# A fused layer (projections, attention, expert layer) on one core: the first attention group's operands loaded during the projections, and most of the expert choice made there too

## The chip, the cores and the metric

One Trainium2 chip, one core of it. The metric is the device time of one execution in microseconds (us). It is given as the median over runs of the same kernel; one further execution was recorded by the hardware profiler, and all rows of the trace come from that one.

## What is computed

```python
xn = _layernorm(x, axis=-1)                     # x: 16 x 1024 x 256
s = _L0_attn_ref(xn, W_q, W_k, W_v, W_o)        # 16 heads of 16, rope on q and k, causal softmax
g = _silu(_L0_ffn_ref(xn, w_router, w_fc, w_proj))
x = x + s * g
# in _L0_ffn_ref:
logits = jnp.einsum('bsd,ed->bse', x, w_router)       # 8 experts
indices = jnp.argmax(softmax(logits), axis=-1)        # the first of the largest
onehot = jax.nn.one_hot(indices, NUM_EXPERTS)
```

Every token goes to one expert out of eight, the first that has its largest logit.

## The kernel before

The program has three stages, each in a block of its own; at the end of a block all engines wait for each other.

**Projections** (`project_phase`). The 16384 tokens are 32 tiles (t) of 512 tokens, and each tile is 4 subtiles of 128 tokens, 128 subtiles (n) in all. For each tile: ScalarE (ACT) applies the layer norm (`apply`, L278), TensorE (PE) transposes, ACT and VectorE (DVE) cut the result in two parts (`xT_hi` L286, `xT_lo` L354). For each subtile PE makes v, the eight logits (ps_vr) and q, k (ps_qk) in three passes each; DVE does the rope products (L385 to L387), GpSimd (POOL) adds them (L263), PE transposes the sum, and ACT, DVE and POOL cut it in three bf16 parts (`part1` L300, `take_rest` L395, `part2` L306, `part3` L252). q and k leave for DRAM as `parts_dram`, v as `v_dram`, the normed tokens as `xn_dram`, and zeros go to `xs_dram`.

The order on each engine is written out by hand. All these transfers are issued by SyncE (SP), in one loop over tiles: store xn of t+1, load x of t+4, one or two stores of zeros, wait for v of t, store it (L203, 4 transfers), wait for `part3` of t, store the parts (L206, 4 transfers). Most buffers are double: ACT's v copy for tile t waits for the v store of tile t-2 (`v_stored`), and `part1` for tile t waits for the parts store of tile t-2 (`parts_stored`). DVE's loop does, for subtile n: `xT_lo` of the next tile when n is a tile's last subtile, `rope_parts(n)`, `ln_stats`, `take_rest(n-2)`, and at a tile's last subtile the layer norm's means and variances, from which POOL makes the factors that `apply` waits for.

After the loop DVE chooses the experts of all 16384 tokens in one go (L415 to L426: largest logit, which experts equal it, their numbers, the lowest, a 0/1 table `onehot`). PE counts from `onehot`, and DVE works out each token's place in the sorted order (L432 to L467, to `slot` and `block_expert`). With that the block ends.

**Attention** (`attention_phase`). 64 groups (16 batches by 4 groups of 4 heads), with operand buffers q_st, k_st, v_st in a ring of four. `load(b, r)` brings one group's operands with 13 transfers: 6 for q and 6 for k, each of 16 partitions and 128 KB, and one of 512 KB over 128 partitions for v. At the block's start SP issues the loads of groups 0, 1 and 2, and then `load_max(0, 0, 0)`, which waits for the first maxima. PE waits for POOL's constants (`a_consts`) and for group 0's 13 transfers, and then forms the 32 row blocks of group 0 (L947), whose maxima DVE takes (L855); the steady loop over groups begins after them. POOL's setting of ones in k_st is waited for only after those 32.

**Experts and output** (`expert_output_phase`) is untouched.

## Time and profile before

| | us |
|---|---|
| median of 3 runs (lowest, highest) | 2686.38 (2682.7, 2691.24) |
| the profiled execution: its time | 2684.91 |
| the profiled execution: span of the trace | 2683.2 |
| projections: last PE matmul of the loop ends at about | 408.2 |
| DVE chooses experts, then places | 409.44 to 430.46 |
| attention's block: SP's first load is issued at | 430.75 |
| PE's first matmul of attention | 446.19 |
| steady loop over the 64 groups begins | 473.91 |
| last exponential of attention begins | 2290.6 |
| PE busy, DVE busy over the span | 94%, 80% |

How to read it: times within the trace count from the span's start. The profiled execution's time is 1.7 us more than its span (work around it that no row shows). The page's second part gives, for 40 equal slices of the span, each engine's busy share and TensorE's granted clock; the seventh slice (402 to 470) holds the passage from the projections to attention: PE falls to 3 tenths there, ACT to 0 and the granted clock to 5 tenths. A row with L and a number names the line of the kernel; PEld is PE's weight load, SPq the issuing of a transfer by SP.

### The profile page before, as it was taken

To read this page: it belongs to the slowest core of one execution; us is meant where nothing else is said; L and a number is where in the kernel's file an instruction comes from. 1 tells how busy PE (TensorE), PEld (TensorE's weight loads), DVE (VectorE), ACT (ScalarE), POOL (GpSimd) and SP (SyncE) were. 2 spreads that over 40 slices of the span, in tenths; PEclk is the share of its full clock that TensorE was granted. 3 is DMA by queue.
4 is the path that set the end of the run, shared out by engine and by line. 5 is a ranking of instruction groups with operands and counts; after the bars stand their busy time and mean duration, and the time that the engine had idled before them with its cause. 6 is when DMAs were issued, how large, how long until landed. Compare 5 with 4: busy or idle time off the path is not lost. (4 is left out here: it accounts for less than half of the span.)

```text
span 2683.2 us, 53569 instructions
## 1 busy us (share of the span) xinstructions
PE 2528.3 (94%) x16877; PEld 1271.1 (47%) x16877; DVE 2135.9 (80%) x6183; ACT 1781.9 (66%) x4187; POOL 990.7 (37%) x1189
## 2 busy tenths in 40 slices
PE   7999993999999999999999999999999999799587
PEld 6888781333333333333333333333333333588476
DVE  7888886888888888888888888888888887354244
ACT  5777770677777777777777777777777777455111
POOL 6888883222222222222222222222222222222664
PEclk9999995999999999999999999999999999899798
DMA  6999998456465465454554554654655640697797
GB/s 235 351 350 354 347 336 184 98 103 121 88 111 105 91 111 110 95 115 94 101 122 88 106 110 88 111 112 94 112 98 99 116 96 24 214 307 260 234 339 253
DMA packets 305865, 435.04 MB, mean 162 GB/s; under 512 B 101808, under 2 KB 204464, under 8 KB 305584
## 3 DMA queue, kind: packets, MB, share of 16 engines
q1 hardware_dynamic: 293296, 398.05, 57.6%
q0 software_dynamic: 12288, 33.57, 5.4%
q8 instruction: 136, 2.23, 0.4%
q14 instruction: 145, 1.19, 0.2%
HBM read 241.18 MB, written 188.74 MB: 160 GB/s over the span
## 5 line engine op out<-in xcount | busy, mean ns | idle before, releaser
L855 DVE CUSTOM_DVE_ANT_0 dump<-ps_rows,mask 128x512 bf16<-128x512 f32 (+7 forms) x2048 | 1481.0, 754 | 223.8 <-issue 184.3
L834 ACT ACTIVATE probs<-ps_cols 128x512 f32<-128x512 f32 (+3 forms) x3072 | 1315.7, 495 | 514.2 <-PE ps_cols L1003 504.0
L1003 PE MATMUL ps_cols<-q_st,k_st 99*128 99x512 bf16 (+3 forms) x3072 | 863.0, 329 | 5.5 <-DMA q_st<-max_T 3.3
L813 POOL TENSOR_SCALAR_AFFINE_SELECT probs<-probs 128x512 f32<-128x512 f32 x512 | 325.9, 636 | 1363.1 <-ACT probs L834 1363.1
L947 PE MATMUL ps_rows<-k_st,q_st 96*128 96x512 bf16 (+3 forms) x3072 | 781.5, 330 | 29.8 <-DMA v_st<-v_dram 22.1
L979 PE MATMUL ps_ctx<-probs,v_st 128*32 128x512 f32 (+3 forms) x6144 | 654.5, 498 | 1.5 <-POOL probs L813 1.2
L1003 PEld LDWEIGHTS ps_cols<-q_st,k_st 99*128 99x128 bf16 x3072 | 279.7, 97 | 590.4 <-ACT probs L834 380.3
L947 PEld LDWEIGHTS ps_rows<-k_st,q_st 96*128 96x128 bf16 x3072 | 265.3, 98 | 326.8 <-DVE row_max L855 128.0
L979 PEld LDWEIGHTS ps_ctx<-probs,v_st 128*32 128x32 f32 x6144 | 120.8, 108 | 206.2 <-issue 103.0
L263 POOL TENSOR_TENSOR roped<-rope_c,rope_s 128x512 f32<-128x512 f32 x128 | 164.9, 1288 | 41.8 <-DVE rope_s L387 41.8
L855 DVE DVE_READ_ACCUMULATOR2_ANT row_max<- 128x1 f32 x2048 | 168.2, 82 | 0.2
L1295 PE MATMUL ps_t<-w_o_sb,cT 128*128 128x256 f32 x512 | 130.8, 408 | 38.4 <-issue 22.3
L1165 POOL DMA_INDIRECT gate<-g_dram,slot x128 | 127.8, 998 | 74.5 <-issue 36.3
L252 POOL TENSOR_TENSOR parts<-rest,parts 128x512 bf16<-128x512 f32 x128 | 149.4, 1168 | 1.2 <-ACT parts L306 1.2
L1236 DVE TENSOR_TENSOR prod<-ps_t,gate 128x512 f32<-128x512 f32 x64 | 43.0, 688 | 133.8 <-remote 74.8
L1206 ACT ACTIVATE cT<-ps_t 128x512 f32<-128x512 f32 x64 | 34.9, 598 | 168.4 <-remote 86.5
L800 POOL DMA_INDIRECT xs_dram<-xn_sb,slot x128 | 124.5, 973 | 31.3 <-issue 31.3
L1295 PEld LDWEIGHTS ps_t<-w_o_sb,cT 128*128 128x128 f32 x512 | 102.6, 205 | 57.2 <-issue 27.9
L395 DVE TENSOR_TENSOR rest<-ps_m,parts 128x512 f32<-128x512 f32 x128 | 87.3, 682 | 47.5 <-ACT parts L300 46.4
L485 PE MATMUL ps_qk<-w_all_hi,xT_hi 128*128 128x512 f32 x256 | 101.9, 398 | 0.0
L485 PE MATMUL ps_vr<-w_all_hi,xT_hi 128*128 128x264 f32 x256 | 84.7, 331 | 18.0 <-DVE xT_lo L354 17.9
L485 PE MATMUL ps_qk<-w_all_lo,xT_hi 128*128 128x512 f32 x256 | 101.6, 397 | 0.0
(115 smaller groups left out, 2639.5 us busy)
## 6 DMA issues: line engine op xcount, KB each, us to landing
parts_dram<-parts SPq DMA_DIRECT2D x128, 384.0 KB, 3.9
q_st<-parts_dram SPq DMA_DIRECT2D x384, 128.0 KB
k_st<-parts_dram SPq DMA_DIRECT2D x384, 128.0 KB
v_dram<-v_sb SPq DMA_DIRECT2D x128, 256.0 KB, 5.4
v_st<-v_dram SPq DMA_DIRECT2D x64, 512.0 KB
xs_dram<-zeros SPq DMA_DIRECT2D x36, 512.0 KB, 7.0
xs_sb<-xs_dram SPq DMA_DIRECT2D x72, 256.0 KB, 4.5
g_dram<-g_sb SPq DMA_DIRECT2D x72, 256.0 KB, 3.4
```

The costliest lines, as they stand in the source:

```text
L252: nc.gpsimd.tensor_tensor(parts[:, t % 2, :, 2, s * P:(s + 1) * P], rest[:, n % RR].rearrange("p (b t) -> p b t", b=4), parts[:, t % 2, :, ...
L263: nc.gpsimd.tensor_tensor(roped[:, n % RR, :], rope_c[:, n % 2, :], rope_s[:, n % 2, :], ALU.add).then_inc(roped_ready, 1)
L485: mm = nc.tensor.matmul(out, lhs(i, c), rhs(j, c), start=((c, i, j) == PASSES[0]), stop=((c, i, j) == PASSES[-1]))
L800: pool.indirect_dma_start(out=xs_dram[:, :], out_offset=bass.IndirectOffsetOnAxis(ap=token_row[:, s:s + 1], axis=0), in_=xn_sb[:, u, s % S ...
L813: nc.gpsimd.affine_select(out=tri, in_=tri, compare_op=ALU.is_ge, fill=0.0, base=0, pattern=[[0, GH], [1, P]], channel_multiplier=-1).then ...
L834: nc.scalar.activation(probs[:, k % PB, h, 0:w], ps_cols[(GH * k + h) % CB][:, 0:w], ACT.Exp).then_inc(exp_done, 1)
L855: nc.vector.tensor_tensor_reduce(out=dump[:, even, 0:n], in0=ps_rows[:, 512 * bank:512 * bank + n], in1=mask[:, S - n:S], scale=1.0, scala ...
L947: mm = nc.tensor.matmul(ps_rows[:, 512 * (bank + c):512 * (bank + c) + w], q, k_st[r][0:KS, c, h * 512:h * 512 + w], start=True, stop=True)
L979: mm = nc.tensor.matmul(ps_ctx[VW * h:VW * (h + 1), o:o + w], v_st[r][:, j, VW * h:VW * (h + 1)], probs[:, k % PB, h, 0:w], start=(j == 0) ...
L1003: nc.tensor.matmul(ps_cols[(GH * k + h) % CB][:, 0:w], k_st[r][:, j // IB, h * 512 + (j % IB) * P:h * 512 + (j % IB + 1) * P], q_st[r][:, ...
L1165: pool.indirect_dma_start(out=gate[:, r, s, :], out_offset=None, in_=g_dram[:, :], in_offset=bass.IndirectOffsetOnAxis(ap=token_row[:, t * ...
L1295: mm = nc.tensor.matmul(ps_y[u][i][:, (s % 2) * D:(s % 2 + 1) * D], cT[:, u, c, s * P:(s + 1) * P], w_o_sb[:, c, :], start=(c == 0), stop= ...
```

## The change

Two things are moved, both out of the passage between the two blocks.

1. Group 0's operand buffers (`q_st0`, `k_st0`, `v_st0`) and their semaphore live for the whole program. SP issues group 0's 13 loads in the projections' loop, in the pass for tile 8, between that tile's v stores and its parts stores; it first waits until the stores of tiles 0 and 1 are done. At the start of attention's block SP issues only the loads of groups 1 and 2. Before the first block ends SP waits for group 0's loads.
2. The expert choice is a helper `choose(i, lo, hi, done)` of five steps. The steps for subtiles 0 to 111 (the first 28 tiles) are put into DVE's loop, one after each `take_rest` of subtiles 112 to 116; the steps for the last 16 subtiles come after the loop. `onehot` is now written expert by expert, so that its innermost run is contiguous.

```diff
+def load_operands(sp, parts_dram, v_dram, b, r, q, k, v, loaded):
+
+    for a, (dst, slots) in enumerate(((q, SLOT_Q), (k, SLOT_K))):
+        for slot, part in enumerate(slots):
+            src = parts_dram[:, 2 * a + r // 2, part, (r % 2) * GW:(r % 2 + 1) * GW, :].rearrange(
+                "(b c) (d h) t -> b d c (h t)", c=TPB, h=GH)[b]
+            sp.dma_start(dst[slot * HD:(slot + 1) * HD], src).then_inc(loaded, 16)
+    src = v_dram[:, r].rearrange("(b c) p n -> b p c n", c=TPB)[b]
+    sp.dma_start(v[:].rearrange("p (c s) n -> p c (s n)", c=TPB), src).then_inc(loaded, 16)
...
+    FIRST_GROUP_AT = 8
+    EARLY = (NT - 4) * SUB
+    CHOICE = 5
+    ROUTED = 1 + 2 * CHOICE
...
+            if t == FIRST_GROUP_AT:
+                for j in range(TPB):
+                    sp.wait_ge(v_stored[j % 2], 16 * NG * (j // 2 + 1))
+                    sp.wait_ge(parts_stored[j % 2], 64 * (j // 2 + 1))
+                load_operands(sp, parts_dram, v_dram, 0, 0, *first_in)
             sp.wait_ge(part3_done, SUB * (t + 1))
...
+        sp.wait_ge(first_in[3], LOAD)
         sp.wait_ge(xs_cleared, 16 * CLEARS)
...
+        nc.vector.tensor_scalar_add(ids_low[:], ids_sb[:], -float(E)).then_inc(route, 1)
+
+        def choose(i, lo, hi, done):
+
+            w = hi - lo
+            ids = ids_low[:].unsqueeze(1).broadcast_to((P, w, E))
+            dve.wait_ge(route, done)
+            if i == 0:
+                dve.wait_ge(logits_ready, hi)
+                nc.vector.tensor_reduce(best[:, lo:hi], logits[:, lo:hi], axis=mybir.AxisListType.X,
+                                        op=ALU.max).then_inc(route, 1)
+            elif i == 1:
+                nc.vector.tensor_tensor(is_best[:, lo:hi], logits[:, lo:hi],
+                                        best[:, lo:hi].unsqueeze(2).broadcast_to((P, w, E)),
+                                        ALU.is_equal).then_inc(route, 1)
+            elif i == 2:
+                nc.vector.tensor_tensor(is_best[:, lo:hi], is_best[:, lo:hi], ids, ALU.mult).then_inc(route, 1)
+            elif i == 3:
+                nc.vector.tensor_reduce(first_best[:, lo:hi], is_best[:, lo:hi], axis=mybir.AxisListType.X,
+                                        op=ALU.min).then_inc(route, 1)
+            else:
+                nc.vector.tensor_tensor(onehot[:, :, lo:hi], first_best[:, lo:hi].unsqueeze(1).broadcast_to((P, E, w)),
+                                        ids_low[:].unsqueeze(2).broadcast_to((P, E, w)),
+                                        ALU.is_equal).then_inc(route, 1)
...
             if n >= LAG:
                 take_rest(n - LAG)
+            if EARLY <= n - 2 < EARLY + CHOICE:
+                choose(n - 2 - EARLY, 0, EARLY, 1 + n - 2 - EARLY)
...
+        for i in range(CHOICE):
+            choose(i, EARLY, NS, 1 + CHOICE + i)
...
-        for r in range(RING - 1):
+        for r in range(1, RING - 1):
             load(0, r)
```

The removed lines of the choice are in the kernel above (L414 to L428). Nothing else is changed but numbers of semaphore waits.

How the order moves, at the three places that the prediction speaks of. The line numbers after the change are higher by the lines added above.

**SP in the projections, the pass for tile 8.** Before, from that tile's v stores (L203) to the next tile's:

```order
L203 DMA v_dram<-v_sb 128x512 x4
L206 DMA parts_dram<-parts 128x3x512 x4
L175 DMA xn_dram<-xn 128x1024
L172 DMA x_sb<-in_x_dram 128x4x256
L178 DMA xs_dram<-zeros 128x1024
L203 DMA v_dram<-v_sb 128x512 x4
```

Now:

```order
L231 DMA v_dram<-v_sb 128x512 x4
L79 DMA q_st<-parts_dram 16x2x2048 x6
L79 DMA k_st<-parts_dram 16x2x2048 x6
L81 DMA v_st<-v_dram 128x2x512
L239 DMA parts_dram<-parts 128x3x512 x4
L203 DMA xn_dram<-xn 128x1024
L200 DMA x_sb<-in_x_dram 128x4x256
L206 DMA xs_dram<-zeros 128x1024
L231 DMA v_dram<-v_sb 128x512 x4
```

Thirteen transfers stand ahead of tile 8's parts stores, in the same queue.

**DVE in the projections, end of tile 28 and tile 29** (xT_lo is what PE waits for at a tile's start). Now, from the first choice step on:

```order
L442 TENSOR_REDUCE best<-logits 128x112
L388 TENSOR_TENSOR xT_lo<-ps_f,xT_hi 128x512 x2
...
L429 TENSOR_TENSOR rest<-ps_m,parts 128x512
L445 TENSOR_TENSOR is_best<-logits,best 128x896
L377 BN_AGGR mv<-stats 128x2 x4
...
L429 TENSOR_TENSOR rest<-ps_m,parts 128x512
L449 TENSOR_TENSOR is_best<-is_best,ids_low 128x896
...
L429 TENSOR_TENSOR rest<-ps_m,parts 128x512
L451 TENSOR_REDUCE first_best<-is_best 128x112
...
L429 TENSOR_TENSOR rest<-ps_m,parts 128x512
L454 TENSOR_TENSOR onehot<-first_best,ids_low 128x8x112
L388 TENSOR_TENSOR xT_lo<-ps_f,xT_hi 128x512 x2
```

Five instructions are new there: one ahead of xT_lo of tile 29, one ahead of the means (BN_AGGR) of tile 30, and three more ahead of xT_lo of tile 30. Before, none of them stood there.

**DVE after the projections' loop.** Before:

```order
L395 TENSOR_TENSOR rest<-ps_m,parts 128x512 x3
L415 TENSOR_REDUCE best<-logits 128x128
L416 TENSOR_SCALAR ids_low<-ids_sb 128x8
L418 TENSOR_TENSOR is_best<-logits,best 128x1024
L421 TENSOR_TENSOR is_best<-is_best,ids_low 128x1024
L424 TENSOR_REDUCE first_best<-is_best 128x128
L426 TENSOR_TENSOR onehot<-first_best,ids_low 128x128x8
L432 CAST sub_total<-ps_f 128x8
```

Now:

```order
L429 TENSOR_TENSOR rest<-ps_m,parts 128x512 x3
L442 TENSOR_REDUCE best<-logits 128x16
L445 TENSOR_TENSOR is_best<-logits,best 128x128
L449 TENSOR_TENSOR is_best<-is_best,ids_low 128x128
L451 TENSOR_REDUCE first_best<-is_best 128x16
L454 TENSOR_TENSOR onehot<-first_best,ids_low 128x8x16
L479 CAST sub_total<-ps_f 128x8
```

The same five steps remain, over an eighth of the elements; ids_low has left.

## Rows read from the trace of the kernel before

**Rows 1.** The page, busy time of each engine over the span

```profile
PE 2528.3 (94%) x16877; PEld 1271.1 (47%) x16877; DVE 2135.9 (80%) x6183; ACT 1781.9 (66%) x4187; POOL 990.7 (37%) x1189
```

**Rows 2.** Windows: from:to, length, busy PE PEld DVE ACT POOL, PEclk, DMA share, GB/s

```profile
137.93:150.10 12.17, 11.65 (x73) 9.86 (x73) 10.67 (x29) 8.88 (x23) 10.81 (x11) 1.00 1.03 367
```

**Rows 3.** Timeline after the projections: start, duration, engine, line, operation [idle before]

```profile
407.43 4.49 POOL L252 TENSOR_TENSOR parts<-rest,parts 128x512 bf16<-128x512 f32 x4
...
409.44 1.21 DVE L415 TENSOR_REDUCE best<-logits 128x128 f32<-128x1024 f32 x1
...
410.87 2.13 DVE L418 TENSOR_TENSOR is_best<-logits,best 128x1024 f32<-128x1024 f32 x1
413.03 1.22 DVE L421 TENSOR_TENSOR is_best<-is_best,ids_low 128x1024 f32<-128x1024 f32 x1
...
415.54 4.70 DVE L426 TENSOR_TENSOR onehot<-first_best,ids_low 128x1024 bf16<-128x1024 f32 x1
...
430.23 0.23 DVE L467 CAST slot<-best 128x128 uint32<-128x128 f32 x1
```

**Rows 4.** Timeline, the last stores and the start of attention's block

```profile
413.97 3.25 SPq L206 DMA_DIRECT2D parts_dram<-parts  x4
...
430.75 2.67 SPq L727 DMA_DIRECT2D q_st<-parts_dram  x6
...
432.64 0.29 POOL L789 TENSOR_SCALAR_AFFINE_SELECT ident_b<-ident_b 128x128 bf16<-128x128 bf16 x1
...
446.19 6.89 PE L947 MATMUL ps_rows<-k_st,q_st 96*128 96x512 bf16 x16 [22.11 <-DMA v_st<-v_dram]
...
471.37 0.95 SPq L739 DMA_DIRECT2D q_st<-max_T  x1
```

**Rows 5.** Windows: group 0's q and k loads, then its v load

```profile
431.60:443.90 12.30, 0.00 (x0) 0.00 (x0) 0.00 (x0) 0.00 (x0) 12.09 (x10) 0.50 1.04 141
443.90:445.50 1.60, 0.00 (x0) 0.00 (x0) 0.00 (x0) 0.00 (x0) 1.60 (x1) 0.50 1.23 355
```

**Rows 6.** Timeline of SP's queue, the pass for tile 8

```profile
132.01 3.96 SPq L203 DMA_DIRECT2D v_dram<-v_sb  x4
138.34 2.34 SPq L206 DMA_DIRECT2D parts_dram<-parts  x4
```

**Rows 7.** Timeline of ACT in tile 10: v copy, part1 of its first subtile

```profile
141.04 0.39 ACT L319 ACTIVATE v_sb<-ps_vr 128x256 f32<-128x256 f32 x1 [1.90 <-DMA v_dram<-v_sb]
...
147.09 0.60 ACT L300 ACTIVATE parts<-ps_m 128x512 bf16<-128x512 f32 x1 [0.30 <-PE ps_m L494]
```

**Rows 8.** Timeline of tile 25, from its first PE matmul to that of tile 26

```profile
320.35 0.39 PE L485 MATMUL ps_vr<-w_all_hi,xT_hi 128*128 128x264 f32 x1 [0.46 <-DVE xT_lo L354]
...
325.55 0.38 ACT L319 ACTIVATE v_sb<-ps_vr 128x256 f32<-128x256 f32 x1 [3.99 <-DMA v_dram<-v_sb]
...
333.88 0.39 PE L485 MATMUL ps_vr<-w_all_hi,xT_hi 128*128 128x264 f32 x1 [0.48 <-DVE xT_lo L354]
```

**Rows 9.** Windows: the granted clock (PEclk) after the projections

```profile
411.00:413.00 2.00, 0.00 (x0) 0.00 (x0) 2.00 (x1) 0.00 (x0) 0.92 (x1) 0.50 1.06 429
446.00:454.00 8.00, 6.99 (x18) 1.92 (x19) 6.77 (x32) 0.00 (x0) 0.86 (x1) 0.50 1.06 136
474.00:475.00 1.00, 1.00 (x3) 0.34 (x4) 0.00 (x0) 0.44 (x1) 0.00 (x0) 0.50 0.88 352
478.00:479.00 1.00, 1.00 (x8) 0.35 (x6) 1.00 (x6) 0.73 (x2) 0.49 (x1) 0.73 0.00 0
```

**Rows 10.** Timeline of DVE, small and contiguous operations of the placing

```profile
420.91 1.23 DVE L435 TENSOR_TENSOR before_sub<-earlier,sub_total 128x1024 bf16<-128x1024 bf16 x1
...
423.49 0.22 DVE L444 TENSOR_TENSOR lower_n<-lower_e,n_blocks 128x64 f32<-128x64 f32 x1
423.75 0.22 DVE L447 TENSOR_REDUCE first_block<-lower_n 128x8 f32<-128x64 f32 x1
```

**Rows 11.** Timeline, start of tile 29: DVE's xT_lo and PE's first matmul

```profile
369.01 1.28 DVE L354 TENSOR_TENSOR xT_lo<-ps_f,xT_hi 128x512 fp32r<-128x512 f32 x2
...
370.34 0.39 PE L485 MATMUL ps_vr<-w_all_hi,xT_hi 128*128 128x264 f32 x1 [0.47 <-DVE xT_lo L354]
```

More of the change, by code:

```diff
@@ L412, in _ @@
                 ln_variance(t + 2)
-        dve.wait_ge(logits_ready, NS)
-        nc.vector.tensor_reduce(best[:], logits[:], axis=mybir.AxisListType.X, op=ALU.max).then_inc(route, 1)
-        nc.vector.tensor_scalar_add(ids_low[:], ids_sb[:], -float(E)).then_inc(route, 1)
-        dve.wait_ge(route, 2)
-        nc.vector.tensor_tensor(is_best[:], logits[:], best[:].unsqueeze(2).broadcast_to((P, NS, E)),
-                                ALU.is_equal).then_inc(route, 1)
-        dve.wait_ge(route, 3)
-        nc.vector.tensor_tensor(is_best[:], is_best[:], ids_low[:].unsqueeze(1).broadcast_to((P, NS, E)),
-                                ALU.mult).then_inc(route, 1)
-        dve.wait_ge(route, 4)
-        nc.vector.tensor_reduce(first_best[:], is_best[:], axis=mybir.AxisListType.X, op=ALU.min).then_inc(route, 1)
-        dve.wait_ge(route, 5)
-        nc.vector.tensor_tensor(onehot[:].rearrange("p e s -> p s e"),
-                                first_best[:].unsqueeze(2).broadcast_to((P, NS, E)),
-                                ids_low[:].unsqueeze(1).broadcast_to((P, NS, E)), ALU.is_equal).then_inc(route, 1)
-        ROUTED = 6
+        for i in range(CHOICE):
+            choose(i, EARLY, NS, 1 + CHOICE + i)
         dve.wait_ge(totals_ready, 1)
@@ L519, in _ @@
                 transpose_qk(n - LAG)
-        pe.wait_ge(route, 6)
+        pe.wait_ge(route, ROUTED)
         pe.wait_ge(consts_ready, CONSTS)
@@ L534, in _, with attention_phase @@
                              start=False, stop=True).then_inc(ranks_ready, 1)
-def attention_phase(nc, ctx, parts_dram, v_dram, ctx_dram, xn_dram, xs_dram, token_row):
+def attention_phase(nc, ctx, parts_dram, v_dram, ctx_dram, xn_dram, xs_dram, token_row, first_in):
     def sb(name, shape, dt=F32):
@@ L556, in attention_phase @@
     RING = NG
-    KM = KS + PARTS
     HALVES = S // 512
     IB = 512 // P
-    q_st = [sb(f"q_st{r}", [KM, HALVES, GH * 512], BF16) for r in range(RING)]
-    k_st = [sb(f"k_st{r}", [KM, HALVES, GH * 512], BF16) for r in range(RING)]
-    v_st = [sb(f"v_st{r}", [P, NB, GH * VW]) for r in range(RING)]
+    q_st = [first_in[0]] + [sb(f"q_st{r}", [KM, HALVES, GH * 512], BF16) for r in range(1, RING)]
+    k_st = [first_in[1]] + [sb(f"k_st{r}", [KM, HALVES, GH * 512], BF16) for r in range(1, RING)]
+    v_st = [first_in[2]] + [sb(f"v_st{r}", [P, NB, GH * VW]) for r in range(1, RING)]
     mask = sb("mask", [P, S])
@@ L586, in attention_phase @@
     ones_set = sem("ones_set")
-    operands_loaded = [sem(f"operands_loaded{r}") for r in range(RING)]
+    operands_loaded = [first_in[3]] + [sem(f"operands_loaded{r}") for r in range(1, RING)]
     slot_ready = sem("slot_ready")
@@ L713, in attention_phase @@
     block = ctx.enter_context(nc.Block())
-    LOAD = 16 * (2 * len(SLOT_Q) + 1)
     SUBS_SCATTERED = NT * SUB // N
@@ L720, in load @@
         def load(b, r):
-            done = operands_loaded[r]
-            for a, (dst, slots) in enumerate(((q_st[r], SLOT_Q), (k_st[r], SLOT_K))):
-                for slot, part in enumerate(slots):
-                    src = parts_dram[:, 2 * a + r // 2, part, (r % 2) * GW:(r % 2 + 1) * GW, :].rearrange(
-                        "(b c) (d h) t -> b d c (h t)", c=TPB, h=GH)[b]
-                    sp.dma_start(dst[slot * HD:(slot + 1) * HD], src).then_inc(done, 16)
-            src = v_dram[:, r].rearrange("(b c) p n -> b p c n", c=TPB)[b]
-            sp.dma_start(v_st[r][:].rearrange("p (c s) n -> p c (s n)", c=TPB), src).then_inc(done, 16)
+            load_operands(sp, parts_dram, v_dram, b, r, q_st[r], k_st[r], v_st[r], operands_loaded[r])
         def load_max(n, r, c):
@@ L1332, in gated_attention @@
         token_row, block_expert = routing_tables(nc, whole)
+        first_in = first_operands(nc, whole)
         with ExitStack() as ctx:
             project_phase(nc, ctx, x_t, w_all, rope, expert_ids, parts_dram, v_dram, xn_dram, xs_dram,
-                          (token_row, block_expert))
+                          (token_row, block_expert), first_in)
         with ExitStack() as ctx:
-            attention_phase(nc, ctx, parts_dram, v_dram, ctx_dram, xn_dram, xs_dram, token_row)
+            attention_phase(nc, ctx, parts_dram, v_dram, ctx_dram, xn_dram, xs_dram, token_row, first_in)
         with ExitStack() as ctx:
```

14 lines of the change are left out of this document (11 added, 3 removed).

## The prediction

> **What bounds the kernel now.** I read the page first: PE is busy 94% of the span [rows 1], so a gain has to come from a stretch where PE stands idle, and anything that delays PE inside a dense stretch is paid in full. Then the windows: in tile 10 of the projections PE is busy 11.65 of 12.17 us, DVE 10.67, POOL 10.81, and the DMA share is 1.03 at 367 GB/s [rows 2]. So PE sets the pace there and everything else, the DMA engines too, has little to spare. Then the timeline of the passage: DVE begins the choice at 409.44, and its last operation ends at 430.46 (430.23 + 0.23) [rows 3]; SP's first load goes out at 430.75, and PE's first matmul of attention starts at 446.19 with "DMA v_st<-v_dram" as the releaser of its wait [rows 4]. These are two serial pieces of 21 and 15.4 us with PE nearly idle, and the change takes something from both. What it takes it puts into the dense stretch, so the question is what it costs there.
>
> **The load, where it leaves.** Without group 0's load PE starts when POOL's constants are ready, 432.64 + 0.29 = 432.93, which is 2.2 us after the block's start instead of 15.4. **Saved: 446.19 - 432.93 = 13.2 us.** What comes next is not late: the 32 row blocks and the copy of the maxima take 471.37 - 446.19 = 25.2 us whatever starts them [rows 4], so SP would issue the first maxima at 2.2 + 25.2 = 27.4 us after the block's start, and the loads of groups 1 and 2, 13.9 us each (below), would end at 0.85 + 27.8 = 28.6. That bounds a new wait by 1.2 us; I take 0, since the maxima's transfer itself is small.
>
> **The load, where it arrives.** Its price on the DMA engines: q and k pass from 431.60 to 443.90 at 141 GB/s with the share at 1.04, v from 443.90 to 445.50 at 355 GB/s [rows 5]. So the load fills all engines for 12.3 + 1.6 = 13.9 us, though it is only 2.1 MB; at the 367 GB/s of tile 10 it would be 5.7 us. The twelve q and k transfers, of 16 partitions each, are the slow ones. One page explains it: the Trainium skill, "SBUF — State Buffer", section "Door 1: The DMA port swizzle", says that a transfer reaches only the ports that its partitions belong to, that 16 partitions reach 4 of 16 ports, about 109 GB/s. The trace agrees in kind, with 141 where the page has 109 (successive transfers go to other partitions). By the page's figure alone the load would hold the engines 16.0 us and my sum would come out 2.1 us later.
>
> In the changed kernel these 13 transfers are issued behind tile 8's v stores, which end at 132.01 + 3.96 = 135.97 [rows 6], in the one queue that SP has. Those v stores have landed at 141.04, when ACT's wait for them ends [rows 7], so the engines are at the new load between 136 and 140; I take 138.5 and get 152.4 for its end. Tile 8's parts stores (issued at 138.34 before [rows 6]; 1.6 MB, 4 us at 367 to 400 GB/s) come next and land, with 1 us that I allow for the end of a store, at 157.4. `part1` of tile 10 waits for them, and it started at 147.09 [rows 7]. **ACT is held for 10.3 us.** Nothing on ACT can pass it: behind it stand xT_hi of tile 11 and the v copies, and PE waits for xT at every tile's start even now (0.47 us [rows 11]), so PE loses 10.3 too. Such lateness is handed on: in tile 25 the v store came late, ACT waited 3.99 us [rows 8] instead of 1.90 [rows 7], and the tile took 333.88 - 320.35 = 13.5 us [rows 8] instead of 12.2. Bounds: 7.5 us if the load starts at 136 and shares a little with the stores, 13 us if it starts at 140 and later v stores are late too. SP's own issuing, 6 us for 13 transfers at 2.67 us for six [rows 4], lies beneath this.
>
> The clock adds to it. PE's last matmul of the projections ended at about 408.2 and from 411 on the granted clock is 0.50, 1.2 GHz [rows 9]. After PE starts in earnest at 473.9 it stays at 0.50 and is back at 2.4 GHz within the window 478 to 479 (0.73) [rows 9]: 4.4 us at half speed, 2.2 us of work lost. A stall of 10 us will do the same to a stage that PE bounds: **2.2 us**, between 0 (the stall falls in pieces) and 11.7 (a whole tile at half speed, below).
>
> Load in all: -13.2 + 10.3 + 2.2 = **-0.7 us**.
>
> **The choice, where it leaves.** It took 420.24 - 409.44 = 10.8 us. Five steps over 16 subtiles (128 elements a partition) remain. Neighbouring steps over 64 elements start 0.26 us apart (423.49, 423.75 [rows 10]); a further 64 elements add 0.07 by the 1.22 us of 1024 [rows 3], so five steps are 1.7 us. The 4.70 us of `onehot` [rows 3] belonged to its scattered bf16 writing; contiguous, the like operation took 1.23 us [rows 10], and I count `onehot` as an ordinary step. But POOL is in its last four L252 until 411.92, and the same rows show what that does [rows 3]: is_best, with two inputs in SBUF, was on the engine from 410.87 for 2.13 us and ended at 413.00, which is 1.08 after POOL's end; the mult of the same size after it took 1.22. The reduce before it (one input) ran its usual 1.21 beside POOL. In the new order two such steps meet POOL, so I take 2.8 us instead of 1.7 (ends: 1.7, and 3.8 if DVE waits for all four). **Saved: 10.8 - 2.8 = 8.0 us** (7.0 to 9.1). The 10.2 us of placing are unchanged, so the block ends near 422.8 on the old clock; SP's last stores, issued by 417.22 [rows 4], are done a few us later and stay just ahead.
>
> **The choice, where it arrives.** Five steps over 896 elements, 7/8 of 1.22 less the overlap of neighbours, 1.0 us each: 5.0 us of DVE work in tiles 28 and 29. At 369.01 DVE begins xT_lo of tile 29 directly after a `rest`, and PE, at 370.34, had waited 0.47 us for it [rows 11]. The first step stands exactly before it, the second before the means that POOL and ACT wait for before PE's next transposes, the other three before xT_lo of tile 30, in a stretch where DVE has no gap. So I count them as paid in full, 5.0 us. Three have two SBUF inputs and meet POOL, which is busy 10.81 of 12.17 us [rows 2]: from 0 to 1.2 us for each (the 1.05 that is_best lost beside POOL [rows 3] is one such), I take 0.5: 1.5 us. The same page, section "Who interferes with whom", has it that the pair of ports is held for a whole instruction and that POOL is stopped by DVE as well; no row here shows that side. **Paid: 6.5 us** (5.0 to 8.6). ids_low at the start (0.3 us) lies under PE's first matmuls: 0.
>
> Choice in all: -8.0 + 6.5 = **-1.5 us**.
>
> **Sum:** -0.7 - 1.5 = -2.2 us on the profiled execution's 2684.9, 2682.7. The median of the runs lies 1.5 above that execution, so I forecast **2684.2 us**. With all ends together: -13.2 + 7.5 + 5.0 - 9.1 = -9.8, and -13.2 + 13 + 2.2 + 8.6 - 7.0 = +3.6, so 2676.6 to 2690.0. A measurement of this kernel tells about 0.3% (8.1 us) from no change.
>
> **Rivals.**
> - *The load hides.* If the engines are not as full as a share of 1.03 says (ACT waits 1.90 us for a v store without harm [rows 7], and tile 10's 367 GB/s is below the 429 of 411 to 413 [rows 9]), or if stores pass while q and k wait on the receiving side, PE loses some 2 us and the clock stays up: -13.2 + 2 - 1.5 = -12.7, **2673.7**. Such a reading has a page behind it: the Trainium skill, "DMA: Bandwidth & Descriptors", section "Anatomy of one DMA — SWDGE (gpsimd) path", fits 436 GB/s plus about 2 us for a transfer (on POOL's path), which would make the load 4.8 us of engine time, hence nearly free. Against it stands 141 GB/s at a full share with nothing else running [rows 5]. Chance 0.22.
> - *The early steps of the choice hide, the rest as forecast.* If DVE's lateness falls into gaps behind tile 30, where the statistics end, only 1 of 6.5 us is paid: 2684.2 - 5.5 = **2678.7**. Against: PE does not get lost time back, having no gaps. Chance 0.10.
> - *The clock stays down* (slower). In the row blocks PE ran at 0.50 for 28 us though busy 6.99 of 8 us [rows 9]. If the stall in tile 11 leaves PE at 1.2 GHz and waits for late v stores keep it there, each tile costs 11.7 us more [rows 2]. With one and a half tiles: -13.2 + 10.3 + 17.5 - 1.5 = +13.1, **2699.5**. It decides against the change by more than 8.1 us from about one tile on. Against: at half speed PE is busy without a break, as at 474, where the clock came back in 4.4 us. Chance 0.10.
> - *Forecast:* chance 0.58.
>
> **Numbers.** Faster by over 0.3%: the load hiding (0.22), part of the second rival (0.04), and the low tail of the forecast (0.05), 0.31. Slower: the clock (0.10) and a tail of 0.01, 0.11. The same: 0.58. The range reaches down to 2672 to take in most of the first rival, and up to 2692; outside are the clock's case and the deeper part of the hiding, some 2 in 10.
>
> **What would show it.** In the changed kernel's trace: the first L947 matmul 2.2 us after SP's first load of the block (else step one is wrong); ACT's L300 of tile 10 idle some 10 us for "DMA parts_dram" and a tile of over 20 us there, with a granted clock of 0.50 after it (if the tile is under 15 us, the load hides); tiles 28 and 29 together 5 to 8.6 us longer; from the first late choice step to PE's count 1.7 to 3.8 us. The forecast is wrong if the sum of the projections' lengthening is under 10 or over 25 us.

## The result, and the profile after

The changed kernel takes 2681.88 us (median of 20 runs, 2678.71 to 2687.96) against 2686.81 (20 runs, 2680.96 to 2691.24) for the kernel before in the same comparison: a ratio of 0.9984 with a 95% interval from 0.9977 to 0.9992, 0.16% or some 4 us less. The interval leaves out 1, so the gain is there, but it is small: it lies within the 0.3% that the prediction calls "the same", and 2.3 us below the forecast of 2684.2. Its profiled execution has a span of 2678.4 us, 4.8 less than before.

The page, busy time of each engine over the span, reads as before [rows 1]; no engine's work has grown by more than 2.2 us:

```profile
PE 2527.3 (94%) x16876; PEld 1272.4 (48%) x16877; DVE 2136.9 (80%) x6188; ACT 1782.4 (67%) x4187; POOL 992.9 (37%) x1189
```

**Where the load arrives.** The timeline of SP's queue, the pass for tile 8 (against [rows 6]):

```profile
130.52 3.75 SPq L231 DMA_DIRECT2D v_dram<-v_sb  x4
134.45 3.83 SPq L79 DMA_DIRECT2D q_st<-parts_dram  x6
138.33 2.76 SPq L79 DMA_DIRECT2D k_st<-parts_dram  x6
141.13 0.43 SPq L81 DMA_DIRECT2D v_st<-v_dram  x1
141.60 2.66 SPq L239 DMA_DIRECT2D parts_dram<-parts  x4
```

ACT in tile 10 (against [rows 7]):

```profile
139.51 0.39 ACT L353 ACTIVATE v_sb<-ps_vr 128x256 f32<-128x256 f32 x1 [1.85 <-DMA v_dram<-v_sb]
...
152.19 0.60 ACT L334 ACTIVATE parts<-ps_m 128x512 bf16<-128x512 f32 x1 [6.88 <-DMA parts_dram<-parts]
```

Windows (the columns of [rows 2]): first over the times of [rows 2], then while q and k pass, then after them:

```profile
137.93:150.10 12.17, 10.16 (x64) 8.40 (x63) 7.34 (x22) 5.14 (x13) 9.48 (x9) 1.00 1.06 279
...
138.30:146.30 8.00, 7.95 (x54) 6.84 (x53) 6.50 (x20) 5.14 (x13) 7.55 (x8) 1.00 1.04 227
146.30:152.20 5.90, 1.84 (x11) 1.28 (x9) 0.47 (x2) 0.01 (x1) 1.55 (x2) 0.92 1.08 391
```

PE's first matmul of tile 11, and the granted clock during its wait:

```profile
155.17 0.59 PE L532 MATMUL ps_vr<-w_all_hi,xT_hi 128*128 128x264 f32 x1 [7.03 <-DVE xT_lo L388]
```

```profile
151.00:152.00 1.00, 0.00 (x0) 0.00 (x0) 0.00 (x0) 0.00 (x0) 0.00 (x0) 0.63 1.03 402
152.00:153.00 1.00, 0.00 (x0) 0.00 (x0) 0.18 (x1) 0.81 (x2) 0.00 (x0) 0.50 1.07 390
```

What to see: 13 issues stand before the parts stores, and these go out at 141.60. Counted from PE's first matmul of tile 10 (137.93 before, 136.46 now) that is 5.1 us, where it was 0.4: 4.7 us late. (The traces are 1.5 us apart: tile 0 took 12.0 us instead of 13.3, and the loop began 0.2 us earlier. Tile 0 takes 12.0 to 13.4 in executions of kernels that don't differ there.) Then their landing takes a median of 7.7 us from the issue instead of 4.2. ACT was ready at 145.3 and waits 6.88 us, and PE, which needs the next tile's xT, waits 7.03. The DMA share stays over 1 in these windows, but with q and k in the queue only 227 GB/s pass; from 146.3 on it is 391 again. From first matmul to first matmul tile 10 takes 18.71 us and tile 11 13.17, where all their neighbours take 12.15: 6.56 + 1.02 = 7.6 us.

**Where the choice arrives.** Timeline, DVE in tiles 28 and 29:

```profile
374.24 1.07 DVE L442 TENSOR_REDUCE best<-logits 128x112 f32<-128x896 f32 x1
...
378.61 1.47 DVE L445 TENSOR_TENSOR is_best<-logits,best 128x896 f32<-128x896 f32 x1
...
384.27 1.08 DVE L449 TENSOR_TENSOR is_best<-is_best,ids_low 128x896 f32<-128x896 f32 x1
...
387.46 1.07 DVE L451 TENSOR_REDUCE first_best<-is_best 128x112 f32<-128x896 f32 x1
...
390.63 1.46 DVE L454 TENSOR_TENSOR onehot<-first_best,ids_low 128x896 bf16<-128x896 f32 x1
392.01 1.28 DVE L388 TENSOR_TENSOR xT_lo<-ps_f,xT_hi 128x512 fp32r<-128x512 f32 x2
```

POOL beside them, two rows of part3 (the second is of the usual length):

```profile
384.32 2.07 POOL L286 TENSOR_TENSOR parts<-rest,parts 128x512 bf16<-128x512 f32 x1
...
387.95 1.17 POOL L286 TENSOR_TENSOR parts<-rest,parts 128x512 bf16<-128x512 f32 x1
```

PE's three waits that follow, then windows of the clock around the last:

```profile
376.56 0.39 PE L532 MATMUL ps_vr<-w_all_hi,xT_hi 128*128 128x264 f32 x1 [1.46 <-DVE xT_lo L388]
...
382.71 0.93 PE L524 MATMUL ps_f<-ident,xn 128*128 128x128 f32 x4 [1.19 <-ACT xn L312]
...
393.34 0.39 PE L532 MATMUL ps_vr<-w_all_hi,xT_hi 128*128 128x264 f32 x1 [3.70 <-DVE xT_lo L388]
```

```profile
390.00:392.00 2.00, 0.00 (x0) 0.00 (x0) 2.00 (x3) 0.91 (x2) 2.00 (x2) 1.00 0.00 0
392.00:394.00 2.00, 0.66 (x4) 0.66 (x5) 2.00 (x5) 0.00 (x0) 1.11 (x1) 0.90 0.00 0
394.00:396.00 2.00, 2.00 (x8) 1.71 (x8) 1.97 (x10) 0.45 (x2) 1.28 (x1) 0.50 1.05 368
396.00:398.00 2.00, 2.00 (x12) 1.68 (x11) 0.71 (x3) 0.55 (x2) 1.81 (x3) 0.74 1.09 385
```

The five steps take 6.15 us on DVE. The three steps with two SBUF inputs meet POOL: is_best and onehot are stretched to 1.47 and 1.46, and beside mult and onehot POOL's addition needs 2.07 and 2.01 us instead of 1.17. PE, for want of xT_lo, waits 1.46 instead of 0.47, then 1.19 for the normed tokens, then 3.70; after that its granted clock is 0.50 (1.2 GHz) for some 3 us. Tiles 28, 29 and 30 take 13.14, 16.78 and 13.40 us: 6.9 us more.

**Where both leave.** Timeline of DVE after the loop (against [rows 3]), and of POOL's last part3:

```profile
421.57 0.28 DVE L442 TENSOR_REDUCE best<-logits 128x16 f32<-128x128 f32 x1
421.89 1.19 DVE L445 TENSOR_TENSOR is_best<-logits,best 128x128 f32<-128x128 f32 x1
423.11 1.12 DVE L449 TENSOR_TENSOR is_best<-is_best,ids_low 128x128 f32<-128x128 f32 x1
...
424.59 0.29 DVE L454 TENSOR_TENSOR onehot<-first_best,ids_low 128x128 bf16<-128x128 f32 x1
```

```profile
419.55 4.54 POOL L286 TENSOR_TENSOR parts<-rest,parts 128x512 bf16<-128x512 f32 x4
```

The start of attention's block, and its first stretch (against [rows 4]):

```profile
435.40 2.66 SPq L79 DMA_DIRECT2D q_st<-parts_dram  x6
...
437.64 6.91 PE L977 MATMUL ps_rows<-k_st,q_st 96*128 96x512 bf16 x16 [8.92 <-POOL ident_b L819]
437.65 13.89 POOL L824 MEMSET k_st<- 3x4096 bf16 x4
...
447.06 1.03 DVE L898 TENSOR_SCALAR max_parts<-row_max 128x16 bf16<-128x16 f32 x1
448.28 0.17 DVE L901 SCALAR_TENSOR_TENSOR max_rest<-row_max,max_parts 128x16 f32<-128x16 f32 x1
449.52 2.05 DVE L905 TENSOR_SCALAR max_parts<-max_rest 128x16 bf16<-128x16 f32 x1
...
466.23 0.59 PE L1033 MATMUL ps_cols<-q_st,k_st 99*128 99x512 bf16 x1 [3.29 <-DMA q_st<-max_T]
```

The late choice takes 3.31 us instead of 10.8: two of its five steps take four times as long as the others; the second ends at 424.23, just after POOL's four end at 424.09. PE's first matmul comes 2.24 us after SP's first load, instead of 15.4. From it to the steady loop it is 28.59 us, where before it was 27.75; that 0.84 us is new and has a cause of its own (e10).

The balance at the start of the steady loop, 473.94 before and 466.23 now: tile 0 -1.3 (it varies, see above), tiles 10 and 11 +7.6, tile 25 -0.9 (unexplained: 13.5 us before, 12.6 here, 13.4 in e1, 12.15 in e3), tiles 28 to 30 +6.9, choice -7.5, PE's start in the block -13.2, first stretch +0.8, the start of the program -0.2; together -7.8, and 7.7 is what the rows give. Of these 7.7 us the span keeps 4.8. Attention takes 1819.1 us instead of 1818.3, and from its last copy to the end 393.1 instead of 391.0, in code that was not touched. Over nine profiled executions (before, the change, e1 to e3, e6, e10 to e12) attention takes 1817.8 to 1819.2 and the rest 388.9 to 394.5. So a trace shows the passage term by term, and the whole to no better than some 5 us.

### The profile page after: what moved, and what is told of

Read it like the earlier page. It is cut to its first block and busy times, and to the rows that moved or that the text cites. A ratio compares the mean times of both kernels' runs of the same rounds, so it can differ in the third digit from the quotient of the medians.

```text
span 2678.4 us, 53577 instructions
## 1 busy us (share of the span) xinstructions
PE 2527.3 (94%) x16876; PEld 1272.4 (48%) x16877; DVE 2136.9 (80%) x6188; ACT 1782.4 (67%) x4187; POOL 992.9 (37%) x1189
## 3 DMA queue, kind: packets, MB, share of 16 engines
q14 instruction: 146, 1.19, 0.2%
## 5 line engine op out<-in xcount | busy, mean ns | idle before, releaser
L312 ACT ACTIVATE xn<-x_sb,shift,rstd 128x256 f32<-128x256 f32 x128 | 69.8, 597 | 49.9 <-POOL shift L257 49.9
```

## The experiments

My theories after the result: (a) the load's stall is smaller than forecast because narrow transfers pass faster among the stores than at the block's start, and it grows with them; its rival, that bytes or issuing set it; (b) the choice's steps cost their own time plus POOL's; (c) both costs are ones of place, and go if the same work is put elsewhere.

All these kernels but e2, e5 and e12 make the whole choice after the loop, with the new layout of `onehot` ("choice late" below):

```diff
-            if EARLY <= n - 2 < EARLY + CHOICE:
-                choose(n - 2 - EARLY, 0, EARLY, 1 + n - 2 - EARLY)
...
-            choose(i, EARLY, NS, 1 + CHOICE + i)
+            choose(i, 0, NS, 1 + i)
```

**e1_load_only**: the load as in the change, choice late.

> Part 1 of the change alone: group 0's load in the pass for tile 8; all five steps of the choice stay behind the loop, over all 128 subtiles, in the changed form (ids_low early, onehot written in contiguous runs). My theory: tiles 10 and 11 are longer by 7.6 us together as in the changed kernel, PE starts attention 2.2 us after the block's start (13.2 us saved), and the choice takes about 7.0 us instead of 10.8, since the 4.70 us of onehot came from its scattered writing. Sum -13.2 + 7.6 + 0.9 - 3.8 = -8.5 us against before, about 2678. Rival: the moving of the choice is what brings the gain and the load nets nothing beyond its stall, onehot stays at 4 us: then 10 us of choice and about -5 us.

Measured: 2677.90 us (8 runs), ratio 0.9972 [0.996, 0.9984]. Tiles 10 and 11 take 19.55 and 14.34, 9.6 us more; ACT waits 7.71. The late choice takes 7.07 us, and `onehot` in it 1.22. The steady loop begins at 465.73, level with the change. So the load is the half that gains, and without any early step the choice is already 3.7 of 10.8 us shorter: 3.5 by `onehot` (4.70 to 1.22) and the rest by the early ids_low. The stall is 2 us longer than in the change, though the code at tile 8 is the same: one trace of a stall tells its length to no better than that.

**e2_choice_only**: the choice as in the change; all three loads at attention's start.

```diff
-            if t == FIRST_GROUP_AT:
...
-                load_operands(sp, parts_dram, v_dram, 0, 0, *first_in)
...
-        for r in range(1, RING - 1):
+        for r in range(RING - 1):
```

> Part 2 alone: the choice for 28 tiles inside the loop, group 0's load at the start of attention as before. My theory: tiles 28 to 30 are longer by about 6.9 us together and the choice behind the loop is shorter by 7.5, -0.6 us, no change that can be told. The wait for xT_lo at tile 30 is about 3.7 us and the granted clock falls to 0.50 after it. Rival: the lengthening of tiles 28 to 30 in the changed kernel came from the transfers moved, not from DVE: then those tiles stay at 12.2 us and the kernel gains 7.5.

Measured: 2686.19 us (11 runs), ratio 0.9997 [0.9988, 1.0007]. Tiles 28 to 30 take 13.14, 16.77 and 13.27, 6.7 us more, and the late choice takes 3.3: part 2 earns nothing that the times can tell. Its first stretch of attention is 27.75 us.

**e3_load_spread**: one of the 13 transfers in each pass for tiles 8 to 20, choice late.

```diff
-            if t == FIRST_GROUP_AT:
+            if FIRST_GROUP_AT <= t < FIRST_GROUP_AT + LOAD // 16:
...
-                load_operands(sp, parts_dram, v_dram, 0, 0, *first_in)
+                load_operands(sp, parts_dram, v_dram, 0, 0, *first_in, only=t - FIRST_GROUP_AT)
```

> As e1, but the 13 transfers are issued one per tile, in the passes for tiles 8 to 20. My theory: the engines have about 1.4 us to spare in each tile, a transfer of 128 KB over 16 partitions takes about 1 us of them, so ACT never waits for a parts store and all tiles from 8 on stay at 12.2 us: -13.2 + 0.9 - 3.8 = -16 us against before, about 2670. Rival: the engines have nothing to spare (their share is 1.0), the 13.9 us are paid in small pieces, 13 tiles are longer by 0.5 to 1 us each, and the time is that of e1 or worse.

Measured: 2667.34 us (5 runs), ratio 0.9935 [0.9922, 0.9948]; a second set of the same kernel (e11, below) gave 0.9935 again. The window of tile 10, in e3:

```profile
137.93:150.10 12.17, 11.65 (x73) 9.81 (x73) 10.67 (x29) 8.88 (x23) 10.79 (x10) 1.00 1.02 368
```

It is that of before [rows 2]. The same 2.1 MB, in thirteen pieces, cost nothing that the rows of e3 show: every tile after the first takes 12.15 us (in e11 and e10, with the same spread load, a tile or two among the thirteen takes 12.3 to 12.4), and the steady loop begins at 455.69, 18.3 us earlier than before.

**e6_wide**: in the pass for tile 8, twelve transfers of 128 KB and one of 512 KB over 128 partitions into spare buffers; the real load stays at attention's start, choice late. It loads 2.1 MB more than needed.

```diff
-                load_operands(sp, parts_dram, v_dram, 0, 0, *first_in)
+                for i in range(12):
+                    sp.dma_start(spare[:, i], v_dram[i // 8, i // 2 % 4, :, i % 2 * 256:i % 2 * 256 + 256])...
+                sp.dma_start(spare_v[:]..., src)...
```

> In the pass for tile 8, 12 transfers of 128 KB over 128 partitions (rows of v) and one of 512 KB, into spare buffers, stand where the changed kernel has group 0's 13; the real load is at the start of attention as before, the choice as in e1. Bytes and number of transfers are those of the load, only the partitions differ. My theory (the narrow transfers hold the engines): the load passes at 350 to 400 GB/s in about 5.7 us, and tiles 10 and 11 are longer by at most 2.5 us. Rival (what counts is SP's issuing of 13 transfers, which sends tile 8's parts store off 4.7 us later, or the bytes alone): tiles 10 and 11 are longer by 6 to 7.6 us as in the changed kernel.

Measured: one execution, 2691.21 us. Tiles 10 and 11 take 18.66 and 13.28, 7.6 us more: a stall as long as that of the change, with transfers that reach all partitions. My theory (a) fell for the size. ACT, SP's queue and windows, in e6:

```profile
152.42 0.60 ACT L339 ACTIVATE parts<-ps_m 128x512 bf16<-128x512 f32 x1 [6.83 <-DMA parts_dram<-parts]
```

```profile
135.29 5.66 SPq L239 DMA_DIRECT2D spare<-v_dram  x12
...
141.47 3.58 SPq L244 DMA_DIRECT2D parts_dram<-parts  x4
```

```profile
138.00:142.00 4.00, 3.95 (x24) 3.02 (x22) 2.98 (x12) 1.54 (x4) 3.71 (x5) 1.00 1.02 344
142.00:146.00 4.00, 4.00 (x29) 3.69 (x30) 3.52 (x8) 3.59 (x10) 3.81 (x4) 1.00 0.94 261
```

The share falls below 1 here, and 128 KB every 0.47 us is 278 GB/s: SP's issuing may let the engines run dry. That is argued, not shown, for such dips come without the load too (222 GB/s at a share of 0.84 in the window 145 to 146 before). Nor does e6 test the partitions alone: its pieces are rows of 1 KB, where q's and k's are of 4 KB, and it passes at 261 to 344 GB/s and not at the 367 of the stage. What it shows is that transfers over all partitions do not make the stall go away.

**e13_four**: the same bytes as four transfers of 512 KB, to tell issuing from bytes (the diff is against e6).

```diff
-                for i in range(12):
...
+                for i in range(4):
+                    src = v_dram[:, i].rearrange("(b c) p n -> b p c n", c=TPB)[0]
+                    sp.dma_start(spare[:, i], src).then_inc(spare_loaded, 16)
```

> As e6 (the real load stays at attention's start), but the 2.1 MB behind tile 8's v stores are four transfers of 512 KB over 128 partitions instead of thirteen, so SP needs about 0.45 us each, 1.8 us, where e6 needed 6.1 us and the change 7.1 us. If SP's issuing sets the stall, tile 8's parts stores go out only 1.8 us later than without a load; what is left is the 2.1 MB at the 367 GB/s of the stage, 5.7 us less about 1.4 us that part1 had to spare: ACT waits 4 to 4.5 us for them in tile 10, and tile 10 takes 16 to 16.5 us. The rival is that the bytes ahead of the parts stores cost the same however they are issued (the landing of the stores sets it, 6.8 us of wait in e6 and 6.9 in the change): then tile 10 takes 18.5 us again.

Measured: one execution, 2690.11 us. SP and ACT, in e13:

```profile
135.12 2.88 SPq L239 DMA_DIRECT2D spare<-v_dram  x4
138.03 4.06 SPq L242 DMA_DIRECT2D parts_dram<-parts  x4
...
149.26 0.60 ACT L337 ACTIVATE parts<-ps_m 128x512 bf16<-128x512 f32 x1 [3.18 <-DMA parts_dram<-parts]
```

Tile 10 starts at 137.22 here, so the parts stores go out 0.8 us after it, only 0.4 later than before and not 1.8: SP had stood idle from 135.97 to 138.34 before [rows 6], and four issues fit into that. They land after a median of 8.4 us, with 2.1 MB ahead of them in the queue. ACT waits 3.18 us, below the 4 to 4.5 expected, and tiles 10 and 11 take 15.02 and 13.40, 4.1 us more. In rough terms the waits add up: by the lateness of the first issue, the median landing and some 1.4 us that part1 has to spare (an estimate), 0.4 + 4.2 - 1.4 = 3.2 here, and 4.7 + 3.5 - 1.4 = 6.8 in the change. For e6 the same sum gives 4.3 + 2.3 - 1.4 = 5.2, where 6.83 was measured, so it is no law. Of the 7.6 us for thirteen transfers 3.5 are gone when the same bytes are issued in four; the other 4.1 are the bytes and the slower clock after the stall. The 3.5 us are more than the 2 us by which e1 and the change differ, but they rest on one trace each, and e13's rows are of 2 KB and not 1 or 4: how much is issuing and how much the form of the transfers is not separated.

**e7_double**: e1 with twelve more narrow transfers behind the load, into spare buffers (1.6 MB more than needed).

```diff
+                for a in range(2):
+                    for slot, part in enumerate((SLOT_Q, SLOT_K)[a]):
...
+                        sp.dma_start(spare[slot * HD:(slot + 1) * HD, a], src).then_inc(spare_loaded, 16)
```

> As e1, with twelve more transfers of 16 partitions and 128 KB behind the thirteen in the pass for tile 8, the same q and k parts again into a spare buffer. What the second dozen adds is its price without any slack. If narrow transfers hold the engines as long as at attention's start (12.3 us for twelve), tiles 10 and 11 get longer by another 12 us, 21 in all. If they pass faster in the projections (e1's trace has about 215 GB/s while they pass), another 7 to 8 us, 17 in all. If, as in e6, only bytes count (1.57 MB at 385 GB/s), another 4 us.

Measured: one execution, 2651.39 us, with the kernel before at 2648.28 in that comparison. (The chip of that comparison ran the kernel before 1.4% faster: granted clock 0.981, not 0.972. e5, e8 and e9 are from it too. Their times are compared by ratio only; the undisturbed tiles take 12.15 us there as well.) Tile 10 takes 27.13 and tile 11 13.23: 16.1 us more than undisturbed, 6.5 more than e1 and 8.5 more than the change, nearest to the 17 of the second case. ACT and a window, in e7:

```profile
161.93 0.60 ACT L341 ACTIVATE parts<-ps_m 128x512 bf16<-128x512 f32 x1 [15.29 <-DMA parts_dram<-parts]
```

```profile
139.50:155.50 16.00, 9.92 (x63) 8.24 (x62) 7.10 (x21) 5.13 (x13) 9.21 (x9) 0.96 1.05 204
```

Here the 24 narrow transfers, with v's 512 KB among them, fill the queue for 16 us: 204 GB/s at a full share, against 141 of [rows 5]. At 204 GB/s twelve would take 7.7 us. Twelve more cost 6.5 to 8.5 us, where SP needs 5.8 us to issue them, so for the narrow ones passing is probably the limit once enough are queued; the difference is within the 2 us of e1 and the change.

**e9_half**: q's six transfers in the pass for tile 8, the other seven one each in tiles 20 to 26, choice late.

> Only the six q transfers in the pass for tile 8, the other seven one per tile in the passes for tiles 20 to 26. With a fixed slack of some 3.5 us between the parts store's landing and part1, and 8.7 us for thirteen transfers, six take 3.7 us and the stall nearly vanishes: tiles 10 and 11 longer by 0 to 1.5 us. If instead a stall is in proportion to the transfers, 3.5 us.

Measured: one execution, 2634.74 us. ACT waits 3.06 us for the v store (1.90 in [rows 7]) and 1.14 for the parts; tiles 10 and 11 take 13.42 and 12.48, 1.6 us more, at the slack's 0 to 1.5 and not at the 3.5 of mere proportion. Six cost 1.6, thirteen 7.6 to 9.6, 25 16.1: a slack, then 0.9 to 1.1 us for each, and further on 0.5 to 0.7.

**e8_tail**: the 13 transfers are issued behind tile 31's parts stores and the block's end does not wait for them, choice late.

```diff
+        load_operands(sp, parts_dram, v_dram, 0, 0, *first_in)
...
-        sp.wait_ge(first_in[3], LOAD)
```

> The load goes behind tile 31's parts stores, at the end of the projections' block, which does not wait for it; the choice as in e1. My theory: the engines are free from about 420 on, while DVE chooses and places, so no tile gets longer; at 141 GB/s the load ends about 14 us later, at 434, and PE starts attention there instead of at 446.2: with the choice shorter by 3.8 us the block starts at 427 and PE waits another 7 us for the load. -12 us against before. If the load is as quick as in e1 (about 9 us), -16 us. Rival: it holds up something of the block's end, or the loads of groups 1 and 2 behind it delay the maxima: -8 us.

Measured: 2637.93 us (5 runs), ratio 0.9955 [0.9942, 0.9969]. All tiles after the first take 12.15 us. PE, in e8, whose block's first load is issued at 425.11:

```profile
433.09 6.89 PE L969 MATMUL ps_rows<-k_st,q_st 96*128 96x512 bf16 x16 [14.65 <-DMA v_st<-v_dram]
```

PE starts 8.0 us into the block instead of 15.4: half of the wait is gone at no price in the projections. The load stands behind the last stores in the queue and passes slowly after them (380 GB/s in the window 416 to 419, 128 from 419 to 422).

**e5_both**: e3 with the choice of the first 26 tiles in five steps, each ahead of a `take_rest` in tiles 27 to 31, where I had seen DVE wait for ACT, and the rest after the loop.

```diff
+            if n >= 109 and n < 109 + SUB * CHOICE and n % SUB == 1:
+                choose((n - 109) // SUB, 0, EARLY, 1 + (n - 109) // SUB)
             if n >= LAG:
                 take_rest(n - LAG)
```

> The spread load of e3, and the choice for the first 26 tiles made in five steps, each ahead of the rest of a tile's second subtile, where DVE idles 1.43 us for part1 (tiles 27 to 31); the last 24 subtiles' choice behind the loop. My theory: a step of 0.9 us fits into a gap of 1.43 us and costs nothing, so tiles 27 to 31 stay within 1 us together of 12.15 each, and the choice behind the loop takes 3.7 us instead of 7.1: 3 us less than e3, ratio to before about 0.992. Rival: the three steps with two SBUF inputs wait for POOL there, up to 1.2 us each, which overruns the gap, and POOL is held too: 2 to 4 us are paid and the kernel is level with e3.

Measured: 2635.34 us (5 runs), ratio 0.995 [0.9937, 0.9964]. Tiles 27 to 30 take 12.95, 13.94, 14.20 and 12.29, 4.8 us more in all. A step and what POOL did beside it, in e5:

```profile
364.93 1.99 DVE L450 TENSOR_TENSOR is_best<-logits,best 128x832 f32<-128x832 f32 x1
```

```profile
365.99 1.96 POOL L291 TENSOR_TENSOR parts<-rest,parts 128x512 bf16<-128x512 f32 x1
```

The step meets POOL, takes 1.99 us instead of 1.0, and then holds POOL in turn; the gap of 1.43 us was shorter than that. The steps were not hidden: the rival came true.

**e11_spread_again** and **e12_both_again**: e3 and e5 once more, on one chip.

> The same kernel as e3, for a comparison with e12 on one chip: ratio to the kernel before 0.9935 as there, within 0.9922 to 0.9948, stretch of the first row blocks 28.6 us.

> The same kernel as e5. By the trace of e5 the early steps of the choice cost 4.8 us in the projections and save 3.5 us behind them, so it should be 1.3 us, 0.05%, slower than e11: a ratio of 0.994. If the two lie more than 0.15% apart (e5 showed 0.995 on another chip than e3's 0.9935), something else than the passage and the projections differs between them, and the rows of attention would have to show it.

Measured: e11 2668.49 us, ratio 0.9935 [0.9922, 0.9949]; e12 2670.35, ratio 0.9946 [0.9932, 0.996]. They lie 0.07% apart by the medians and 0.11% by the ratios, which 5 runs each don't tell from level; the start of the steady loop, 455.18 and 456.62, says that e12 is 1.4 us behind.

**e10_ones_late**: e3, with POOL's setting of ones held back until DVE has split the first maxima.

```diff
+        pool.wait_ge(max_chain, MAX_OPS)
         for r in range(RING):
             nc.gpsimd.memset(k_st[r][KS:KM], 1.0).then_inc(ones_set, 1)
```

> The spread load (as e3), and POOL's four memsets of ones in k_st wait until DVE has split the first half's maxima (its four small operations), so they run some 12 to 26 us after PE's first matmul of attention. My theory is that the 0.9 us by which the first 32 row blocks grew wherever PE starts 2.2 us into the block (28.59 instead of 27.72 us from PE's first matmul to the steady loop) comes from two small DVE operations that stand still until a memset ends. By it the stretch is 27.7 us here, the two small operations take 0.2 us each, and the kernel gains 0.9 us over e11, too little for the times to tell. The rival is that the stretch grew because PE and DVE start while the loads of groups 1 and 2 pass: then it stays at 28.6. A second risk is that the memsets, ending some 27 us after PE's first matmul, are late for the steady loop; then PE would show a wait for POOL there.

Measured: 2667.6 us (5 runs), ratio 0.9938 [0.9925, 0.9952]. In e10:

```profile
427.98 6.91 PE L980 MATMUL ps_rows<-k_st,q_st 96*128 96x512 bf16 x16 [8.91 <-POOL ident_b L821]
...
437.39 0.17 DVE L901 TENSOR_SCALAR max_parts<-row_max 128x16 bf16<-128x16 f32 x1
...
439.85 0.17 DVE L908 TENSOR_SCALAR max_parts<-max_rest 128x16 bf16<-128x16 f32 x1
...
455.75 0.58 PE L1036 MATMUL ps_cols<-q_st,k_st 99*128 99x512 bf16 x1 [3.29 <-DMA q_st<-max_T]
```

Both operations take 0.17 us, and the stretch 27.77 us, where e11 has 28.56 (e3 28.59). The 0.8 us was theirs; the loads of groups 1 and 2 pass in e10 as well and did not keep the stretch long. PE does not wait for POOL at the steady loop either (its wait is the 3.29 us for max_T as before). In the time of the kernel the gain is too little to see.

**Best version:** e3 (e11 and e10 are level with it), 17.5 us (0.65%) below the kernel before, and 13 us, 0.5%, below the change by the ratios (0.9935 against 0.9984, intervals apart). At the steady loop the rows have 10.5 of these 13 us (455.69 against 466.23).

## Why the prediction was right, and where its steps were not

The number was near (2684.2 forecast, 2681.9 measured) and in the change's own trace both halves have the forecast sign: the load -5.6 us (-0.7 was forecast), the choice -0.6 (-1.5). Step by step:

- *Load, where it leaves: -13.2.* Held: PE starts 2.24 us after SP's first load. The sentence that the first stretch takes the same "whatever starts them" failed: +0.84 us, for a reason I had not looked for.
- *Load, where it arrives: 10.3 us of stall.* The mechanism held (ACT, part1 of tile 10, waiting for tile 8's parts stores), the term was mis-sized: 6.88 us, and tile 10 took 18.7 us, not the "over 20" of the signs. Two figures in it failed. The 13.9 us of engine time, taken from the block's start, is too long here: going by the rate of the queue, which rises from 227 to 391 GB/s at about 146.3, q and k are through there, and v's 512 KB, at that rate, 1.3 us later: 147.6 by this estimate, where 152.4 was forecast (150.9 in this trace's time). And "SP's own issuing lies beneath this" is not so: the 13 issues send the parts stores off 4.7 us late, and the same bytes in four issues cost 4.1 us instead of 7.6 (e13, with the reserve named there).
- *The narrow transfers.* By the Trainium skill, "SBUF — State Buffer", section "Door 1: The DMA port swizzle", 16 partitions reach a quarter of the ports, 109 GB/s. The traces agree in kind: the share is full at 128 to 141 GB/s where narrow transfers pass behind the projections, and at 194 to 227 in them, against 391 for wide ones. They do not agree in size. The rule would have made the stall larger still.
- *Clock after the stall: 2.2.* Mis-sized, if tile 11's lengthening is taken for it: 1.0 in the change, 1.1 in e7, 2.2 in e1, 1.3 in e13. PE ran at 0.50 for about 2.9 us in the change (155.2 to 158.1) and 5.5 in e1, where 4.4 was forecast. The clock came back within tile 11 in each, so the slower rival did not happen.
- *Choice, where it leaves: -8.0.* Measured -7.5: two steps met POOL as I had counted, but waited 0.9 and 0.8 us: 3.3 us in all, between the 2.8 taken and the upper end of 3.8.
- *Choice, where it arrives: +6.5.* Measured +6.9, in e2 +6.7. Its parts were others than mine: 6.15 us of DVE, POOL held in turn for 0.9 and 0.8 us, and a clock loss of some 1.2 us that I had not counted; against that PE waits for less than DVE's whole lateness. The premise that DVE "has no gap" in that stretch was wrong, as this row of before, in tile 29, shows (e5 shows that such a gap did not help):

```profile
376.05 0.69 DVE L395 TENSOR_TENSOR rest<-ps_m,parts 128x512 f32<-128x512 f32 x1 [1.43 <-ACT parts L300]
```

- *Rivals.* "The load hides" is false for the load in one piece, and true for it in thirteen (e3). "The early steps hide" is false, also where DVE had gaps (e5).
- *Sum.* The terms I forecast came to -2.2 us; the same terms measured come to -13.2 + 7.6 - 7.5 + 6.9 + 0.8 = -5.4, close to the -4.9 of the medians. That the total came so near is in part luck: the load's arrival was 4.9 us too dear in the forecast, the choice 0.9 too cheap, the 0.8 of the first stretch was not foreseen, and the untouched stages differ by up to 1.4 and 5.6 us from trace to trace. The "wrong if" bound of 10 to 25 us for the projections' lengthening held: 7.6 + 6.9 = 14.5.

Left open: why narrow transfers pass at 141 GB/s or less behind the projections and at about 200 in them. It is neither the block's start (in e8 they pass at 128 to 130 between 419 and 425, before it) nor the stores mixed in (in e7's window 149 to 155, when by the order of the queue only narrow ones pass, it is 194). Their order, size and target partitions are the same; no run changed what else differs.

## What to carry to other kernels

A load moved into a dense stretch costs most by standing as one block ahead of a store that someone waits for (2.1 MB: 7.6 us in thirteen issues, 4.1 in four, nothing when spread): count the issues in that queue as well as the bytes, find the slack of the next waiter, and put in each pass no more than that slack (here one transfer of 13 per tile cost nothing, six at once cost 1.6 us). DVE work put into a stretch bound by PE, with POOL busy beside it, was paid in full or more (6.15 us of it cost 6.9), even in gaps of DVE, where a step with two SBUF inputs met POOL and took 1.99 us instead of 1.0. Before splitting a step over two places, make it cheaper where it stands: writing `onehot` in contiguous runs gave 3.5 us for nothing (e1), the split another 3.8 for 6.7.
